# A metaformer kernel on one core: a new order of all engines up to the experts

## The reference

```python
x = x + L0_conv(ln(x))     # covariance pooling: a gate per image and channel
t = t + L0_ffn(ln(t))      # mixture of 8 experts, top 2 by a router
x = x + L1_conv(ln(x))     # 8 shifted directions, a 64 x 64 product each
t = t + L1_ffn(ln(t))      # 8 experts for all tokens, weighted by one softmax
```

```python
# L0_conv, per image; xs is (64, 256)
cov = xs @ I_hat @ xs.T;  normA = trace(cov);  A = cov / normA
ZY = 0.5 * (3 I - A);  Y = A @ ZY;  Z = ZY
for _ in range(1, 4):
    ZY = 0.5 * (3 I - Z @ Y);  Y = Y @ ZY;  Z = ZY @ Z
y = mean(0.5 * Y @ (3 I - Z @ Y) * sqrt(normA), axis=-1)
gate = sigmoid(conv2(relu(conv1(y))));   out = gate * x
# L0_ffn: logits -> softmax -> top 2 -> weights that sum to 1
h = gelu(tokens @ w1[e] + b1[e]);  y = h @ w2[e] + b2[e];  out += combine[:, e] * y
```

## Time and profile before

| | us |
|---|---|
| median of 3 runs | 350.57 |
| lowest and highest | 348.54, 351.87 |
| the profiled execution | 349.9 |
| its span, first to last instruction | 348.1 |
| PE busy | 289.8 (83%) |
| DVE busy | 225.3 (65%) |
| ACT busy | 154.1 (44%) |
| POOL busy | 139.1 (40%) |

### The profile page before, as it was taken

The page is one execution under the profiler, slowest core; times in us unless marked ns, Lnnn a source line. Parts: engine busy times, 40 slices in busy tenths (PEclk is TensorE's granted clock), DMA queues, the critical chain, the costliest instruction groups (busy, mean ns, idle before and its releaser), DMA issues.

```text
span 348.1 us, 9439 instructions
## 1 busy us (share of the span) xinstructions
PE 289.8 (83%) x3835; PEld 186.0 (53%) x3835; DVE 225.3 (65%) x687; ACT 154.1 (44%) x290; POOL 139.1 (40%) x151
## 2 busy tenths in 40 slices
PE   0467789765388998899878999997889999999995
PEld 0356688652265666666555656663634445444443
DVE  5965335648848877887849689857356545555551
ACT  1686331020426555755464445556145454544430
POOL 6414163525696586410011357877209960000000
PEclk9999958755669999999998999999599999999999
DMA  7233000000469758866872000000000000000001
GB/s 228 73 68 73 4 2 2 2 0 2 122 161 211 175 141 183 211 169 168 196 196 47 4 0 2 3 2 2 1 1 2 2 32 32 32 30 3 32 32 60
DMA packets 16983, 23.54 MB, mean 68 GB/s; under 512 B 8132, under 2 KB 12780, under 8 KB 16940
## 3 DMA queue, kind: packets, MB, share of 16 engines
q1 hardware_dynamic: 16940, 22.94, 26.4%
HBM read 20.57 MB, written 2.36 MB: 66 GB/s over the span
## 4 chain that ended last, share of the span: by engine, by line
PE 45%; DVE 20%; issue 12%; POOL 9%; DMA 8%; SPq 3%; ACT 2%; DVEq 0%; POOLq 0%
PE pair L1758 8%; PE pair L1742 8%; PE pair L1728 7%; DVE scaled L859 4%; POOL ln_rstd L577 4%; DMA hid<-c_dram 3%; DMA c_dram<-cT 3%; PE pair L1640 2%; PE pair L1562 2%; PE pair L1589 2%; PE pair L1401 2%; PE pair L1411 2%; DVE stats L758 2%; POOL xs_sum L591 2%; PE pair L1378 1%
## 5 line engine op out<-in xcount | busy, mean ns | idle before, releaser
L1247 ACT ACTIVATE pair<-pair,cols 128x512 f32<-128x512 f32 x64 | 39.6, 657 | 35.8 <-PE pair L1562 35.8
L1282 ACT ACTIVATE hid<-pair,bn 128x1024 f32<-128x1024 f32 x32 | 38.5, 1202 | 34.7 <-PE pair L1728 34.7
L577 POOL TENSOR_TENSOR ln_rstd<-ln_var,neg_half 128x8 f32<-128x8 f32 x16 | 26.9, 1692 | 55.8 <-DVE ln_var L881 55.8
L1562 PE MATMUL pair<-xs,w1f 64*64 64x256 f32 x512 | 37.2, 410 | 3.6 <-DVE scaled L859 3.5
L1589 PE MATMUL pair<-scaled,w 64*64 64x256 f32 x512 | 37.1, 394 | 0.1
L1728 PE MATMUL pair<-xs_ffn,f1f 64*64 64x512 f32 x256 | 34.3, 606 | 0.9 <-DVE x L896 0.9
L1742 PE MATMUL pair<-hid,f 64*64 64x512 f32 x256 | 34.4, 608 | 0.0
L1640 PE MATMUL pair<-xp,vconv 64*64 64x256 f32 x512 | 32.4, 400 | 0.0
L859 DVE TENSOR_TENSOR scaled<-pair,xs_ffn 128x1024 f32<-128x1024 f32 x16 | 19.5, 1219 | 11.2 <-PE pair L1589 6.7
L859 DVE TENSOR_TENSOR scaled<-pair,hid 128x1024 f32<-128x1024 f32 x16 | 19.5, 1217 | 10.9 <-PE pair L1589 5.6
L1093 DVE SCALAR_TENSOR_TENSOR xn<-pair,neg_shift,ln_x 128x512 f32<-128x512 f32 x24 | 16.9, 746 | 14.5 <-PE pair L1742 14.5
...
## 6 DMA issues: line engine op xcount, KB each, us to landing
...
```

The costliest lines, as they stand in the source:

```text
L577: g.tensor_tensor(ln_rstd[:, st, b % 2, :], ln_var[:, st, b % 2, :], neg_half[:, 0:T2], ALU.pow).then_inc(ln_rstd_ready[st], 1)
L1247: s.activation(h, h, ACT.Gelu, bias=cols[:, e:e + 1]).then_inc(hidden_gelu, 1)
L1282: s.activation(hid1[:, n % 2, :, :], pair_of("layer1", n)[:, :, :], ACT.Relu, scale=bn1[:, 0, k:k + 1], bias=bn1[:, 1, k:k + 1]).then_inc( ...
L1562: last = t.matmul(pair[N % 2][halves(th), i, 2 * P * u:2 * P * (u + 1)], w1f[halves(i), C * e:C * (e + 1)], xs[halves(i), b % 3, 2 * P * t ...
```

## The change

All four engines get a new order up to the experts, and three pieces of work are done in another way.

- DVE: `tok_chain` is cut into its six steps, which are woven with statistics and root steps. Groups 0 and 1 are staggered, group 2 starts before group 1 ends, and between the root steps of groups 2 and 3 now stand gate and sum of block 0, statistics of blocks 0 to 2, `moe_sub(0)`, `moe_mult(0)`, `scale_f2`, route(0) and the first part of route(1). `moe_sub(1)` and `moe_mult(1)` go to POOL, and the copies of `b2sel` and `neg_shift2` to ACT (`bn_copies`).
- PE: `vec_cols` (the transpose of the vectors) goes behind `rows_out(0)`. `moe_x(0)`, `moe_logits(0)`, `moe_first(0, 0)`, `moe_x(1)`, `moe_c(0)` and `moe_logits(1)` stand between the root steps of groups 2 and 3. `moe_first(0, 1)` waits for all four gates.
- Gate: `gate_rows` and `gspread` fall away. `gate_spread` is 8 products of 64 x 64 by 64 with the column of tanh repeated as weights and half a unit matrix as the other operand, into the group's own bank; `gate_out` adds 0.5.
- ACT: one load of the gelu table ahead of `gate_relu(0)`, in place of one for tanh there and one for gelu at the first expert.
- POOL: the constants of the last layer (`bn_powers`, `bn_scales`, the same instructions as before) and the two clearings go between the norms of groups 0 to 2.

In the diff the removed lines of the old orders are left out (they stand in the functions above), and so are the definitions that only give old lines a name (`tok_inv` to `tok_shares`, `bn_powers`, `bn_scales`, `vec_cols`, `conv_d`, `conv_c`, `conv_dc`); each line is moved 8 columns to the left.

```diff
@@ -452,54 +451,62 @@
...
+    tok_norm_pool(0, 0)
+    tok_norm_pool(0, 1)
+    tok_norm_pool(1, 0)
+    tok_norm_pool(1, 1)
+    root_of_trace(0)
+    bn_powers()
+    bn_scales()
+    tok_norm_pool(2, 0)
+    tok_norm_pool(2, 1)
+    tok_norm_pool(3, 0)
+    root_of_trace(1)
+    tok_norm_pool(3, 1)
     root_of_trace(2)
     root_of_trace(3)
...
     moe_x1(1)
     moe_rstd(0)
+    moe_resid(0)
+    moe_rstd(1)
+    moe_sub(1)
+    moe_mult(1)
     moe_x1(2)
-    moe_rstd(1)
-    moe_resid(0)
+    moe_resid(1)
     moe_x1(3)
     moe_rstd(2)
     moe_sub(2)
     moe_mult(2)
-    moe_resid(1)
     moe_x1(4)
     moe_rstd(3)
     moe_sub(3)
...
@@ -741,13 +765,6 @@
-    def gate_rows(gr):
-        gs = group(gr)
-        dve.wait_ge(conv2_tanh, gr + 1)
-        v.scalar_tensor_tensor(out=gspread[:, gs, :], in0=over(g2[:, gs], GP), scalar=1.0,
-                               in1=rep(half_ident[:, :].rearrange("p (o c) -> p o c", o=1), 1, GP),
-                               op0=ALU.add, op1=ALU.mult).then_inc(gate_rows_ready, 1)
...
     tok_stats(0, 0, 16)
     tok_aggr(0)
+    tok_stats(1, 0, 4)
+    tok_inv(0)
+    tok_stats(1, 4, 5)
+    tok_over(0)
+    tok_stats(1, 5, 6)
+    tok_twice(0)
+    tok_stats(1, 6, 7)
+    tok_root(0)
+    tok_stats(1, 7, 8)
+    tok_shift(0)
+    tok_stats(1, 8, 9)
+    tok_shares(0)
+    tok_stats(1, 9, 16)
     tok_aggr(1)
+    tok_stats(2, 0, 4)
+    tok_inv(1)
+    tok_stats(2, 4, 5)
+    tok_over(1)
     traces(0)
+    tok_twice(1)
+    tok_stats(2, 5, 6)
+    tok_root(1)
+    tok_stats(2, 6, 7)
+    tok_shift(1)
     dve.wait_ge(ones_set, 1)
     normal(0)
+    tok_shares(1)
+    tok_stats(2, 7, 16)
     take_q(0, 0)
+    tok_aggr(2)
+    take_p(0, 0)
+    traces(1)
+    tok_stats(3, 0, 4)
+    take_q(0, 1)
+    tok_inv(2)
+    tok_stats(3, 4, 5)
+    tok_over(2)
+    tok_stats(3, 5, 6)
+    take_p(0, 1)
+    tok_twice(2)
+    normal(1)
+    tok_root(2)
+    tok_stats(3, 6, 8)
+    tok_shift(2)
+    take_q(0, 2)
+    tok_shares(2)
+    take_q(1, 0)
+    tok_stats(3, 8, 12)
+    take_p(0, 2)
+    take_p(1, 0)
+    tok_stats(3, 12, 16)
+    take_q(0, 3)
+    take_q(1, 1)
     tok_aggr(3)
+    apply_third(0)
+    take_p(1, 1)
+    tok_inv(3)
     traces(2)
+    tok_over(3)
+    apply_fourth(0)
+    tok_twice(3)
+    take_q(1, 2)
+    tok_root(3)
+    tok_shift(3)
+    take_p(1, 2)
+    tok_shares(3)
     normal(2)
     take_q(1, 3)
     traces(3)
+    take_q(2, 0)
     apply_third(1)
     take_p(2, 0)
     x1_gated(0)
+    x1_added(0)
+    apply_fourth(1)
+    normal(3)
+    take_q(2, 1)
+    moe_stats(0)
+    take_q(3, 0)
+    take_p(2, 1)
+    moe_sub(0)
     take_p(3, 0)
+    moe_stats(1)
+    moe_mult(0)
+    scale_f2()
+    take_q(2, 2)
     take_q(3, 1)
+    for part in range(2):
+        route(0, part)
+        take_p(2 + part, 2 - part)
+    take_q(2, 3)
     take_q(3, 2)
+    route(0, 2)
     take_p(3, 2)
+    moe_stats(2)
+    apply_third(2)
     take_q(3, 3)
+    apply_fourth(2)
     apply_third(3)
+    route(1, 0)
     apply_fourth(3)
+    route(1, 1)
     moe_stats(3)
     for b in range(NB - 1):
         if b == 0:
...
@@ -1178,44 +1208,61 @@
...
     def gate_out(gr):
         act_e.wait_ge(gate_in_psum, gr + 1)
-        s.activation(gate[:, group(gr), :].rearrange("p i c -> p (i c)"), bank[4 + gr % 2][:, 0:GP * C], ACT.Copy).then_inc(gate_ready, 1)
+        s.activation(gate[:, group(gr), :].rearrange("p i c -> p (i c)"), bank[gr][:, 0:GP * C], ACT.Identity,
+                     bias=pos_half[:, 0:1]).then_inc(gate_ready, 1)
+    def gate_vectors():
+        act_e.wait_ge(vecs_ready, 1)
+        s.activation(cols[:, :], bank[7][:, 0:NROWS], ACT.Copy).then_inc(cols_ready, 1)
+        act_e.wait_ge(cols_ready, 1)
+        s.activation(half_gb2[:, :], cols[:, ROW_GB2:ROW_GB2 + 1], ACT.Copy, scale=0.5).then_inc(cols_ready, 1)
+    def bn_copies():
+        act_e.wait_ge(bn_step, 11)
+        act_e.wait_ge(own_zero, 1)
+        for half in range(2):
+            flat = b2sel[halves(half), :, :, :].rearrange("p k s e -> p (k s e)")
+            step = 2 * E + 2
+            for part in range(2):
+                first = E * part + half
+                s.activation(flat[:, first:first + (KP - 1) * step + 1:step], bn2[halves(half), 1, :], ACT.Copy).then_inc(b2_sel, 1)
+        for half in range(2):
+            for two in range(2):
+                s.activation(neg_shift2[halves(half), :, two], bn2[halves(two), 2, :], ACT.Copy).then_inc(neg_shift_dup, 1)
     half_std_of(0)
     tok_norm(0)
     half_std_of(1)
     rows_copy(0)
     tok_norm(1)
+    gate_vectors()
+    act_e.wait_ge(conv_wT, 1)
+    for side in range(2):
+        s.activation(wdT[:, :, side, :], bank[6][0:C, :].rearrange("p (d c) -> p d c", d=8), ACT.Copy).then_inc(conv_wTs, 1)
+    rows_copy(1)
     half_std_of(2)
     act_e.wait_ge(conv_wT, 2)
     s.activation(wcT[:, :, :].rearrange("p d c -> p (d c)"), bank[7][0:C, :], ACT.Copy).then_inc(conv_wTs, 1)
+    tok_norm(2)
+    act_e.wait_ge(conv_v, 1)
+    s.activation(vconv[:, :, :], bank[7][:, :].rearrange("p (d o) -> p d o", d=8), ACT.Copy).then_inc(conv_vs, 1)
     act_e.wait_ge(consts_v, 2)
     for i in range(2):
         s.activation(router[halves(i), i, :], cols[halves(i), ROW_ROUTER:ROW_B1], ACT.Copy).then_inc(router_ready, 1)
+    rows_copy(2)
+    half_std_of(3)
+    s.activation(fm[:, 3, :], neg_half[:, 0:2], ACT.Gelu).then_inc(gelu_table, 1)
+    gate_relu(0)
+    tok_norm(3)
+    gate_tanh(0)
+    gate_out(0)
+    rows_copy(3)
+    bn_copies()
     act_e.wait_ge(consts, 20)
     s.activation(sel[:, :, :], sel_f[:, :, :], ACT.Copy).then_inc(w_hi, 1)
     gate_relu(1)
     gate_tanh(1)
     gate_out(1)
     def evac_x(b):
         act_e.wait_ge(tok_T, b + 1)
...
         s.activation(yTf[:, :, :], pair[2][:, :, 0:2 * P], ACT.Copy).then_inc(ffn_y_copied, 1)
     evac_x(0)
+    gelu(0, 0)
+    tanh(0)
+    evac_x(1)
+    c_copy(0)
     gate_relu(2)
+    gate_tanh(2)
     gate_relu(3)
+    gate_out(2)
     gate_tanh(3)
     gate_out(3)
+    tanh(1)
     for b in range(NB):
+        if b:
+            gelu(b, 0)
         if b + 2 < NB:
             evac_x(b + 2)
         if b == NB - 1:
...
@@ -1445,89 +1493,43 @@
     def gate_spread(gr):
-        pe.wait_ge(gate_rows_ready, gr + 1)
-        wait(pe, gate_ready, gr - 1)
+        pe.wait_ge(conv2_tanh, gr + 1)
+        for i in range(GP):
+            for j in range(2):
+                last = t.matmul(bank[gr][halves(j), C * i:C * (i + 1)], rep(g2[halves(j), GP * gr + i:GP * gr + i + 1], 1, C),
+                                half_ident[halves(j), :], start=True, stop=True)
+        last.then_inc(gate_in_psum, 1)
...
+    def second_scale():
+        pe.wait_ge(bn_step, 10)
         pe.wait_ge(rows_T_copied, 2 * NG)
...
+    pe.wait_ge(consts, 20)
+    traces(0)
+    rows_out(0)
+    vec_cols()
+    gram(0)
+    traces(1)
+    conv_d()
+    square(0, 0)
+    conv_c()
+    cube(0, 0)
+    rows_out(1)
+    square(0, 1)
+    cube(0, 1)
+    gram(1)
+    conv_dc()
+    square(0, 2)
+    square(1, 0)
+    traces(2)
+    cube(0, 2)
+    cube(1, 0)
+    square(0, 3)
+    square(1, 1)
+    third(0)
+    rows_out(2)
+    cube(1, 1)
+    fourth(0)
+    square(1, 2)
+    gate_conv1(0)
+    cube(1, 2)
+    gram(2)
+    gate_conv2(0)
+    traces(3)
+    square(1, 3)
+    gate_spread(0)
+    square(2, 0)
+    rows_out(3)
+    third(1)
+    cube(2, 0)
+    fourth(1)
+    square(2, 1)
+    gram(3)
+    gate_conv1(1)
+    square(3, 0)
+    cube(2, 1)
+    gate_conv2(1)
+    cube(3, 0)
+    second_scale()
+    gate_spread(1)
     moe_x(0)
+    square(2, 2)
+    square(3, 1)
     pe.wait_ge(conv_vs, 1)
     pe.wait_ge(router_ready, 2)
     moe_logits(0)
+    pe.wait_ge(w_moe, W_MOE)
+    pe.wait_ge(gate_ready, 2)
+    moe_first(0, 0)
+    cube(2, 2)
+    cube(3, 1)
+    moe_x(1)
+    square(2, 3)
+    square(3, 2)
+    moe_c(0)
+    cube(3, 2)
+    third(2)
+    moe_logits(1)
+    square(3, 3)
+    fourth(2)
+    third(3)
+    gate_conv1(2)
+    fourth(3)
+    gate_conv2(2)
+    gate_conv1(3)
     gate_spread(2)
+    gate_conv2(3)
     gate_spread(3)
+    pe.wait_ge(gate_ready, 4)
     moe_first(0, 1)
+    pe.wait_ge(f2_scaled, 2)
     for b in range(NB):
         if b:
             moe_first(b, 0)
```

296 lines of the change are left out of this document (70 added, 226 removed).

## The result

The changed kernel takes 333.88 us (median of 4 runs, 333.38 to 334.95) against 351.22 us for the kernel before (4 runs of the same session, 348.54 to 354.72): a ratio of 0.955, 95% interval 0.950 to 0.960. The forecast was 330, range 322 to 338. The profiled execution took 334.95 us, its span is 333.2, 14.9 less than before.

The account below looks back on a forecast made before the run. It took the mostly serial 26.1 us between the last root vector and the first routing-weight multiplication as the bound; -22.6, +2.1 and +0.8 gave about 20 us gain, hence 330 us, range 322 to 338.

Parts of the forecast that it names:

- Part 1: Last yv to moe_scale(0, 0): routing and statistics move into VectorE's root gaps, cutting 26.1 us to 3.5, gaining 22.6.
- Part 2: Copies of b2sel and neg_shift2 on ScalarE: bounds nothing and 3.4 us, taken as 1.7 us that relu(1) absorbs.
- Part 3: Run's start: TensorE begins near 12.3 us instead of 13.44; queues walked at 0.57 us per 16 products.
- Part 4: TensorE clock before the experts: first dip gone, another after the wait ahead of moe_x(0); gain 19.7 us at half clock.
- the two walks: Hand walks to moe_scale(1, 0): full clock 82.5 us, gain 27.1; partly half clock 89.9, gain 19.7, the one taken.
- Part 5: ScalarE: one gelu table load before relu(0), 1.28 us delay at most; a drain would cost up to 1.4 us more.
- Part 6: Routing-weight DMA: block 1's spread begins near 82, gaining 20 us, carried through the experts to the end unchanged.
- The sum: Whole kernel: -22.6 tail, +2.1 last yv, +0.8 first block make -19.7; rounded to 20 us gain, about 330 us.
- Rival (a): TensorE clock stays up past moe_x(0): gain 25 to 27 us, time 324 us; chance 15%.
- (b): TensorE clock stays down from 45 to past 90 us, 8 to 10 us more: 339 us; chance 14%.
- (c): Slower than before: head-of-line blocking on VectorE from route(0, 0), 352 to 358 us; chance 4%.
- (d): No change: blocking stalls of 19 to 20 us, or the experts' chain held by DMA; chance 4%.

Follow-up runs that it names:

- u_late: Changed kernel with block statistics, normalisation, logits, routing and first expert product back behind the last root step, plus seven constant products in the last layer: 333.78 us.
- b_copies: Kernel before with only the eight b2sel and neg_shift2 copies moved from VectorE to ScalarE: 351.27 us, ratio 1.000.
- r_after: The changed kernel run again without any edit: 331.40 us, ratio 0.948 to the kernel before.
- a_best: Changed kernel plus seven constant products in the last layer and constant products at the start that also fill TensorE's waits there: 322.71 us, ratio 0.922.
- a_late: Changed kernel plus seven constant products in three TensorE waits at the start of the last layer: 330.38 us, ratio 0.940.
- b_late: Kernel before plus seven constant products in TensorE's waits at the start of the last layer: 349.72 us, ratio 0.996.
- a_mid: Changed kernel plus ten constant products in TensorE's waits between 51 and 72 us: 336.66 us, ratio 0.963.

## Why the prediction was right, and where it was not

**Part 1, the tail.** Forecast 3.5 us behind the last `yv` in place of 26.1; it is 4.46. The step that was short is the wait of 1.14 us for the tanh of route(1) at 76.27: I summed VectorE's own work there and took no latency of ScalarE. That tanh stands behind the gate of group 3, which I priced at 2.4 us and which took 3.8, to the end of its `gate_out`:
```profile
75.66 0.47 ACT L1211 ACTIVATE gate<-pair,pos_half 128x256 f32<-128x256 f32 x1 [1.22 <-PE pair L1499]
76.04 0.20 ACT L1275 ACTIVATE m<-m 128x8 f32<-128x8 f32 x1
```
What the part got wrong is whose the gain is. I gave 3.4 of the 22.6 us to the copies, nothing of its own to the gate spread, and the other 19.2 to the weave, with the last `yv` 2.1 us later. By the tails of the runs the copies are worth 3.1, the gate spread 3.7 and the weave 15.4. u_late shows that without the weave `yv` would come at 60.28, 9.7 us ahead of before, and that the tail would be 19.9, not 26.1. The weave spends 9.3 us of that lead to save 15.4. The net comes out near the forecast; the attribution does not.

**Part 2, the copies.** They take 0.62 + 0.90 = 1.5 us on ScalarE, 3.4 on VectorE before, and stand there:
```profile
46.40 0.62 ACT L1228 ACTIVATE b2sel<-bn 64x4 f32<-64x4 f32 x4
47.04 0.90 ACT L1231 ACTIVATE neg_shift<-bn 64x4 f32<-64x4 f32 x4
...
49.55 0.27 ACT L1202 ACTIVATE g<-pair,cols 128x4 f32<-128x4 f32 x1 [0.96 <-PE pair L1485]
```
I had them delay relu(1) by 1.7 us. The last row is relu(1), and it waited 0.96 us for TensorE with ScalarE idle, so the copies delayed it by nothing, the lower of my two bounds. b_copies gives 3.1 us less tail (26.07 to 23.01), as the forecast's 3.4 of VectorE time had it.

**Part 3, the start.** TensorE's transposes begin at 12.79, forecast 12.3, and `normal(0)` at 17.57, forecast 17.0. Then my walk ran ahead: the gate of group 0 is read at 44.3 (forecast 41), the fourth group's `normal` comes at 49.26 (45.4), the first block is normalised at 54.98 (52.4). The step that failed is the price of a group of 16: 0.57 us, half of the row at 33.20, carried back to the start of the run. There it is 1.13 us, the price of 1.2 GHz, until about 30 us (in the trace of before too, 1.14 at 21.99). The page's clock reads 9 in those slices in both kernels, and I took the line at its word. At full speed too a group that stands alone takes 0.68 us (37.16 after; 27.02 in the trace of before), and 0.57 is half of two in a row.

**Part 4, the clock.** I walked with half clock from 54 to 65 and from 74 to 82. It was half from 67 to 81, and in place of the first stretch stood the slow start. Some 3.3 us late from the start less the stretch that did not come gave 72.22 for the last `yv`, forecast 72.1; 76.68 for `moe_scale(0, 0)`, forecast 75.6; 89.19 for `moe_scale(1, 0)`, forecast 89.9. Right in size, by two errors that cancel, and by luck in one of them: how long the half speed of the start lasts changes from one execution to the next (in r_after it ended at about 25 us and the last `yv` came at 69.98). The weighing of the two walks was right: the stage between 52 and 66 us, with 9.87 of 14 us busy, was followed by one at 0.55. The rule of the Trainium skill, "TensorE: Matmul & The Clock Gate", What's actually happening, that activity releases the throttle, is borne out at the start (a_best). In the last layer a_late agrees and b_late does not, with 0.54 from 252 to 267 us. Nor does a_mid, where 3.72 busy of 4 us did not keep the clock up; in these two the measurement decides.

**Part 5, the table load.** The load and what stands around it on ScalarE after:
```profile
38.00 0.22 ACT L1180 ACTIVATE half_std<-quarter_var 128x16 f32<-128x16 f32 x1
38.23 1.28 ACT L1254 ACT_TABLE_LOAD   x1
39.53 0.20 ACT L1254 ACTIVATE fm<-neg_half 128x2 f32<-128x2 f32 x1
```
It starts 0.01 us after the work ahead of it ends and its user starts 0.02 us behind it: 1.28 us, and none of the drain that the Trainium skill, "ScalarE: Activation LUTs", What ACT_TABLE_LOAD costs, adds.

**Part 6, DMA.** Writes at 65.28 and 81.18 (forecast 65 and 79.8), the spread of block 1 at 82.97 (82), block period 12.05 (11.5 to 12). "Neither grown nor given back" was off by 1.3 us: 20.4 gained at `moe_scale(1, 0)`, 19.1 at the last one. The chain of write, spread and use keeps its period, and it began with a gain of 19.1 (102.03 to 82.97); the lead of `moe_scale(1, 0)` over that was lost on the way.

**The sum.** At block 1 the walk had -22.6, +2.1 and +0.8; the profile has -21.6 (tail), +2.2 (last `yv`) and -1.0, since the first block took 12.5 us and not 14.3. The 1.0 us too much in the one and the 1.8 too little in the other nearly cancel. Forecast 20 us of gain in the profiled execution, measured 14.9: 20.4 at block 1, less 1.3 in the experts, less 4.2 for the second stretch of half clock in the last layer. The last is the term the sum lacked. I had said that the stages after the experts take as long as before. They do in r_after, whose 328.4 us of span are 19.7 under before: the forecast to 0.3 us, and still partly by chance: there block 1 gained 22.4 us and the experts gave 2.7 of it back. Rival (a), a clock that stays up, did not come; (b), half clock from 45 to past 90, did not either; of the head-of-line blocking of (c) there is only the 1.14 us wait; (d) fell.
